# One half of look-ahead more for the first stage, patches in two transfers a unit, and rows doubled by VectorE instead of DMA

## The reference

```python
x = (x - mean) / (1e-06 + std)            # per patch and channel
x = x / math.sqrt(P)
x = _conv2d(x, conv1_w, conv1_b)          # 3 -> 64 channels, 3x3
residual = x
x = _group_norm(x, gn1_g, gn1_b)
x = jax.nn.gelu(x, approximate=False)
x = _conv2d(x, rconv1_w, rconv1_b)        # 64 -> 64, 3x3
x = _group_norm(x, gn2_g, gn2_b)
x = jax.nn.gelu(x, approximate=False)
x = _conv2d(x, rconv2_w, rconv2_b)        # 64 -> 64, 3x3
x = residual + x
x = _conv2d(x, proj_w, proj_b, stride=P, pad=0)   # 64 x 16 x 16 -> 192
```

## Time and profile before

| | us |
|---|---|
| median of 3 runs | 2082.0 |
| lowest, highest | 2076.85, 2090.18 |
| profiled execution, its own time | 2084.01 |
| its span, first to last instruction | 2082.2 |
| mean granted TensorE clock in it | 0.90 |

### The profile page before, as it was taken

The page is one execution under the profiler, slowest core; times in us unless marked ns, Lnnn a source line. Parts: engine busy times, 40 slices in busy tenths (PEclk is TensorE's granted clock), DMA queues, the critical chain, the costliest instruction groups (busy, mean ns, idle before and its releaser), DMA issues. The chain is left out here.

```text
span 2082.2 us, 45356 instructions
## 1 busy us (share of the span) xinstructions
PE 1634.7 (79%) x13560; PEld 1054.4 (51%) x13560; DVE 1224.6 (59%) x4296; ACT 947.6 (46%) x2114; POOL 907.6 (44%) x2183
## 2 busy tenths in 40 slices
PE   7899956777877687777877777687778775798899
PEld 2344423334655455545654555365545554665556
DVE  8876756775656556555665556565565555148240
ACT  3466535554444444444445444444444442032442
POOL 2000036665555555545555555455555552024220
PEclk9999989998989889989998999899888997897789
DMA  5522242223333333333333333333333337620000
GB/s 148 175 83 81 82 172 73 73 73 99 101 92 81 96 92 102 82 91 96 101 84 93 97 94 93 79 104 95 92 86 98 101 90 196 164 50 1 1 1 12
DMA packets 120494, 188.61 MB, mean 91 GB/s; under 512 B 22575, under 2 KB 90350, under 8 KB 120198
## 3 DMA queue, kind: packets, MB, share of 16 engines
q1 hardware_dynamic: 120326, 186.41, 33.5%
HBM read 103.06 MB, written 19.69 MB: 59 GB/s over the span
## 5 line engine op out<-in xcount | busy, mean ns | idle before, releaser
L499 PE MATMUL rc<-sb_acts,sb_rwd 128*64 128x512 f16 x1764 | 651.0, 446 | 336.2 <-DMA sb_acts<-sb_hst 336.1
L500 PE MATMUL rc<-sb_acts,sb_rwd 128*64 128x512 f16 x1764 | 652.2, 446 | 0.0
L414 ACT ACTIVATE sb_f32q<-c,sb_gsh,sb_gsc 128x128 f32<-128x128 f32 x788 | 297.0, 458 | 573.0 <-POOL sb_gsh L368 573.0
L499 PEld LDWEIGHTS rc<-sb_acts,sb_rwd 128*64 128x64 f16 x1764 | 193.1, 124 | 466.5 <-DMA sb_acts<-sb_hst 381.3
L357 POOL TENSOR_TENSOR sb_tmp<-sb_mst 128x4 f32<-128x4 f32 (+1 forms) x296 | 84.6, 286 | 756.3 <-DVE sb_mst L782 756.2
L362 POOL TENSOR_TENSOR sb_tmp<-sb_tmp,sb_half_neg 128x4 f32<-128x4 f32 (+1 forms) x296 | 386.7, 1306 | 23.2
L423 ACT ACTIVATE sb_g2f<-rc,sb_gsh,sb_gsc 128x128 f32<-128x128 f32 x784 | 296.8, 469 | 165.7 <-POOL sb_gsh L368 154.3
L499 PE MATMUL rc<-sb_acts,sb_rwl 128*64 128x512 f16 x1176 | 367.2, 394 | 3.8 <-issue 3.4
L500 PE MATMUL rc<-sb_acts,sb_rwl 128*64 128x512 f16 x1176 | 366.7, 394 | 0.0
L553 PE MATMUL pj<-sb_wall,sb_arena 128*64 128x384 f16 x1792 | 317.7, 357 | 18.8 <-DMA sb_wall<-w_lo 9.9
L782 DVE TENSOR_REDUCE sb_mst<-st 128x8 f32<-128x16 f32 (+1 forms) x296 | 52.6, 178 | 463.0 <-PE st L541 463.0
(11 more groups left out here) (161 smaller groups left out, 2573.8 us busy)
## 6 DMA issues: line engine op xcount, KB each, us to landing
sb_acts<-sb_hst SPq DMA_DIRECT2D x788, 78.8 KB, 2.1
sb_wall<-w_lo SPq DMA_DIRECT2D x56, 528.0 KB, 3.9
sb_im<-x_planes SPq DMA_DIRECT2D x300, 60.7 KB
sb_wall<-w_lo SPq DMA_DIRECT2D x28, 480.0 KB, 3.7
sb_im<-x_planes SPq DMA_DIRECT2D x300, 30.3 KB
sb_f32q<-in_proj SPq DMA_DIRECT2D x12, 576.0 KB, 4.5
sb_arena<-in_proj SPq DMA_DIRECT2D x12, 576.0 KB, 4.8
w_lo<-sb_arena SPq DMA_DIRECT2D x1, 6144.0 KB, 17.0
```

The costliest lines, as they stand in the source:

```text
L414: ins = nc.scalar.activation(g1f[:, q * Q + m, :], c1[q][:, m * HALF:(m + 1) * HALF], ACT.Gelu, bias=gsh[q][:, m:m + 1], scale=gsc[q][:, m ...
L499: nc.tensor.matmul(out[0:CH, :], w_odd, x_odd, start=(n == 0), stop=(n == 14))
L500: yield nc.tensor.matmul(out[CH:128, :], w_even, x_even, start=(n == 0), stop=(n == 14))
```

## The change

**Look-ahead.** The first stage is one half further ahead: in the time of half k, VectorE takes the statistics of half k+3 and splits half k+2, TensorE issues `means` of half k+3 and `conv1` of half k+4, ScalarE does `gelu1` of half k+2. The loop's length is the same; one more half is done in the prologue. `conv1` of half k+4 goes to the bank of the same q, and the wait for a unit's patches moves from q = 1 to q = 0.

**Doubling.** `double` is gone from SyncE. Behind its low part, `split1` copies the two halves of `hst[q]` to both halves of the partitions with four `tensor_copy` of 64 partitions x 630 elements, float16. `split1` no longer waits for transfers out of `hst`. The second-stage moments and `split2` now stand behind these copies.

**Patches.** `x_planes` has 18 planes (high, low, high again) instead of 12, written by three DMAs and six of zeros; `load_im` is two DMAs of 54 partitions instead of three of 24 and three of 12, the same bytes. `w1s` is in that order too, by twelve small DMAs.

```diff
--- before.py
+++ after.py
@@ -36,7 +36,7 @@
 FU = E // U
 RUN = (U - 1) * PAD + 8 * WD + P
 PLANE = (NPAT + 2 * U + 1) * PAD
-KA, KC = 72, 108
+KC = 108
 WS = 64.0
 EPS = 1e-5
 TR = 55
@@ -74,7 +74,7 @@
 
 
 
-    scr = nc.dram_tensor("x_planes", (12, PLANE), F16)
+    scr = nc.dram_tensor("x_planes", (18, PLANE), F16)
     wlod = nc.dram_tensor("w_lo", (128, HALF * E), F16)
     with ExitStack() as ctx:
         def sb(name, shape, dt=F32):
@@ -218,8 +218,9 @@
             sp.dma_start(xt, a["x"].rearrange("c p w n -> p c w n")).then_inc(s_xld, 16)
 
             sp.wait_ge(s_wprep, W_READY)
-            sp.dma_start(w1s[0:KA, :], w1hl[0:KA, 0, :]).then_inc(s_w1s, 16)
-            sp.dma_start(w1s[KA:KC, :], w1hl[KA:KC, 1, :]).then_inc(s_w1s, 16)
+            for at in range(0, KC, 18):
+                sp.dma_start(w1s[at:at + 12, :], w1hl[at:at + 12, 0, :]).then_inc(s_w1s, 16)
+                sp.dma_start(w1s[at + 12:at + 18, :], w1hl[at + 12:at + 18, 1, :]).then_inc(s_w1s, 16)
 
             def fold_io(i, p, last):
                 n = 2 * i + p
@@ -239,26 +240,24 @@
             for c in range(C):
                 sp.dma_start(xs.rearrange("(r w) (c n) -> r c w n", w=7, c=C)[:, c], xt[:, c]).then_inc(s_scr, 16)
             sp.wait_ge(s_xhl, 13)
-            for h in range(2):
-                sp.dma_start(bass.AP(tensor=scr, offset=h * 6 * PLANE, ap=[[7 * PAD, ROWS], [PLANE, 6], [1, 7 * PAD]]),
+            for k, h in enumerate((0, 1, 0)):
+                sp.dma_start(bass.AP(tensor=scr, offset=k * 6 * PLANE, ap=[[7 * PAD, ROWS], [PLANE, 6], [1, 7 * PAD]]),
                              xhl[:, 6 * h:6 * h + 6, :]).then_inc(s_scr, 16)
             sp.wait_ge(s_zero, 1)
             for n, k in ((NPAT, U), (NPAT + U, U), (NPAT + 2 * U, 1)):
-                sp.dma_start(bass.AP(tensor=scr, offset=n * PAD, ap=[[PLANE, 12], [1, k * PAD]]),
-                             zt[:, 0:k * PAD]).then_inc(s_scr, 16)
+                for at, planes in ((0, 12), (12, 6)):
+                    sp.dma_start(bass.AP(tensor=scr, offset=at * PLANE + n * PAD, ap=[[PLANE, planes], [1, k * PAD]]),
+                                 zt[0:planes, 0:k * PAD]).then_inc(s_scr, 16)
             def load_im(u, p):
-                for kx in range(3):
-                    sp.dma_start(im[p][24 * kx:24 * kx + 24, 0:RUN],
-                                 bass.AP(tensor=scr, offset=u * (U * PAD) + kx,
-                                         ap=[[PLANE, 12], [WD, 2], [1, RUN]])).then_inc(s_im[p], 16)
-                    sp.dma_start(im[p][KA + 12 * kx:KA + 12 * kx + 12, 0:RUN],
-                                 bass.AP(tensor=scr, offset=u * (U * PAD) + kx,
-                                         ap=[[PLANE, 6], [WD, 2], [1, RUN]])).then_inc(s_im[p], 16)
+                for up in range(2):
+                    sp.dma_start(im[p][54 * up:54 * up + 54, 0:RUN],
+                                 bass.AP(tensor=scr, offset=u * (U * PAD) + up * WD,
+                                         ap=[[1, 3], [PLANE, 18], [1, RUN]])).then_inc(s_im[p], 16)
 
             with sp.Fori(3, FU // 2 - 1) as i:
                 for p in range(2):
                     fold_io(i, p, False)
-            sp.wait_ge(s_scr, 16 * 8)
+            sp.wait_ge(s_scr, 16 * 12)
             load_im(0, 0)
             load_im(1, 1)
             for p in range(2):
@@ -266,13 +265,6 @@
             sp.wait_ge(s_wlo, 2 * FU)
             sp.dma_start(wlod.ap(), b1[:, 0:HALF * E]).then_inc(s_wst, 16)
             sp.sem_inc(s_emb, 32)
-
-            def double(k, p, q):
-
-                sp.wait_ge(s_sp1h, k + 1)
-                for row, half in ((0, 0), (0, 1), (1, 1), (1, 0)):
-                    sp.dma_start(acts[p][64 * half:64 * half + 64, row, q * Q * PAD + WD:(q + 1) * Q * PAD],
-                                 hst[q][64 * row:64 * row + 64, WD:Q * PAD]).then_inc(s_dup[p][q], 16)
 
             def store_tokens(lo):
                 sp.dma_start(emb[bass.ds(lo, 64), :], tok[0:64, :]).then_inc(s_emb, 16)
@@ -291,15 +283,12 @@
                         u = g * GU + 2 * j + p
                         sp.wait_ge(s_c1, 2 * u + 3)
                         load_im(u + 2, p)
-                        double(2 * u + 1, p, 1)
-                        double(2 * u + 2, 1 - p, 0)
                         if not first and 2 * j + p < NCH:
                             load_chunk(g, 2 * j + p)
                 if not first:
                     sp.wait_ge(s_pjr, g + 1)
                     store_tokens((g - 1) * G)
 
-            double(0, 0, 0)
             over_groups(sp, group)
 
             def load_colour(m):
@@ -332,7 +321,6 @@
             sp.wait_ge(s_pjr, GROUPS + 1)
             store_tokens((GROUPS - 1) * G)
             sp.wait_ge(s_emb, 32 * GROUPS + 32)
-            sp.wait_ge(s_dup[0][0], 64 * (UNITS // 2 + 1))
             sp.wait_ge(s_wr, 32)
 
         @block.gpsimd
@@ -370,14 +358,15 @@
             def pair(u0, j, first):
                 for p in range(2):
                     u = u0 + p
-                    norm(0, 0, 2 * u + 2)
+                    norm(0, 1, 2 * u + 3)
                     if not (first and p == 0):
                         norm(1, N2[1 - p], u - 1)
-                    norm(0, 1, 2 * u + 3)
+                    norm(0, 0, 2 * u + 4)
 
             pool.wait_ge(s_padz, 3)
             norm(0, 0, 0)
             norm(0, 1, 1)
+            norm(0, 0, 2)
             over_groups(pool, lambda g, b, first: over_units(pool, g, pair, first))
             norm(1, N2[1], UNITS - 1)
 
@@ -437,7 +426,7 @@
                         u = u0 + p
                         for q in range(2):
 
-                            gelu1(2 * u + 1 + q, 1 - q, not (first and p == 0 and q == 0))
+                            gelu1(2 * u + 2 + q, q)
                             if first and 2 * p + q < 3:
                                 continue
                             if head and 2 * p + q == 3:
@@ -453,6 +442,7 @@
 
             act.sem_inc(s_g2, 4)
             gelu1(0, 0, False)
+            gelu1(1, 1, False)
             group(0, 0, True)
             act.wait_ge(s_wst, 16)
             with act.Fori(0, (GROUPS - 1) // 2) as i:
@@ -597,15 +587,15 @@
                 woven(6)
                 pe.wait_ge(s_dup[p][q], 64 * (pairs_done + 1))
                 woven(1)
-                means(0, N1[q], 2 * u + q + 2, u - (q == 0) if k2 else 0)
+                means(0, N1[1 - q], 2 * u + q + 3, u - (q == 0) if k2 else 0)
                 woven(3)
-                if q == 1:
-                    pe.wait_ge(s_im[p], 96 * (pairs_done + 2))
-                pe.wait_ge(s_g1, 2 * u + q + 2)
-                conv1(1 - q, 1 - p if q == 0 else p)
+                if q == 0:
+                    pe.wait_ge(s_im[p], 32 * (pairs_done + 2))
+                pe.wait_ge(s_g1, 2 * u + q + 3)
+                conv1(q, p)
                 woven(3)
                 if q == 0 and k2:
-                    means(1, N2[1 - p], u - 1, 2 * u + q + 3)
+                    means(1, N2[1 - p], u - 1, 2 * u + q + 4)
                 woven(2).then_inc(s_rc, 1)
 
             def group0(g, b, first):
@@ -627,20 +617,23 @@
             pe.sem_inc(s_c1, 1)
             pe.sem_inc(s_pc, 2)
             pe.sem_inc(s_pj, 1)
-            pe.wait_ge(s_w1s, 32)
+            pe.wait_ge(s_w1s, 192)
             pe.wait_ge(s_rowz, 4)
-            pe.wait_ge(s_im[0], 96)
+            pe.wait_ge(s_im[0], 32)
             pe.wait_ge(s_tev, 3 * FU)
             pe.wait_ge(s_wlo, 2 * FU)
             conv1(0, 0)
             conv1(1, 0)
             means(0, 0, 0, 0)
             means(0, 1, 1, 0)
-            pe.wait_ge(s_im[1], 96)
+            pe.wait_ge(s_im[1], 32)
             pe.wait_ge(s_g1, 1)
             conv1(0, 1)
+            means(0, 0, 2, 0)
+            pe.wait_ge(s_g1, 2)
+            conv1(1, 1)
             over_groups(pe, group)
-            means(1, N2[1], UNITS - 1, 2 * UNITS + 2)
+            means(1, N2[1], UNITS - 1, 2 * UNITS + 3)
             for c in range(NCH):
                 chunk_waits(GROUPS, c)
                 last = run(project(0, CHS[c], CHS[c] + CHN[c]))
@@ -751,7 +744,7 @@
             ins.then_inc(s_padz, 1)
             dve.wait_ge(s_tps, FU)
             dve.wait_ge(s_padz, 3)
-            dve.wait_ge(s_scr, 16 * 8)
+            dve.wait_ge(s_scr, 16 * 12)
             v.sem_inc(s_rd[0], 1)
             v.sem_inc(s_rd[1], 1)
             v.sem_inc(s_pjr, 1)
@@ -793,6 +786,9 @@
                 v.tensor_copy(hi, src).then_inc(s_sp1h, 1)
                 dve.wait_ge(s_sp1h, k + 1)
                 v.tensor_tensor(lo, src, hi, ALU.subtract).then_inc(s_sp1, 1)
+                for row, half in ((1, 1), (1, 0), (0, 0), (0, 1)):
+                    v.tensor_copy(acts[p][64 * half:64 * half + 64, row, q * Q * PAD + WD:(q + 1) * Q * PAD],
+                                  hst[q][64 * row:64 * row + 64, WD:Q * PAD]).then_inc(s_dup[p][q], 16)
 
             def split2(k, q, buf, slot):
 
```

(22 more changed lines are left out.)

## The result

The changed kernel takes 2204.5 us (median of 4; 2193.5 to 2219.7) beside 2080.4 for the kernel before: ratio 1.059, 95% interval 1.052 to 1.067. Forecast were 1888 us and a range of 1800 to 2020. The change makes the kernel slower, by a mechanism that was not among the rivals. The profiled execution took 2193.5 (span 2191.7), the lowest of the four.

A forecast was written before the change was run, and what follows sets the result against it. TensorE was held by late doubling transfers in SyncE's queue; afterwards VectorE would be fullest. 2082 - 202 (84 units in groups 1 to 6, 15.1 to 12.7 us) + 0 (group 0) + 8 (ends) = 1888 us, range 1800 to 2020.

The forecast's parts named there:

- the price of the patch loads: Patch loads of a unit, covered by about three halves (some 18 us) until conv1: priced at nothing.
- The unit of 12.7 us: A pair of halves in groups 1 to 6, then 15.1 us: 6.6 + 5.5, plus 0.6 for small waits.
- GpSimd's and ScalarE's slack: Three norms need 10 us in 12.7; even half's GELU ends at 12.3, the split wants it at 12.7 + 0.1.
- GpSimd held up by the copies: VectorE's copies keep GpSimd out, three norms grow by up to 2.8 us, unit 14.1: 2020 us; chance 0.13.
- the copy: Each of VectorE's four copies a half, 630 elements on 64 partitions: 0.35 us, near the value by bytes.
- the rival of 1800 us: VectorE's copies cost about 0.24 us each (short and overlapped), unit 11.8 us: 1800 us; chance 0.15.
- those of 0.49 and 0.84: Copy at the CAST's rate (0.49 us): 1999 us, chance 0.12; one element at a time (0.84): 2273, chance 0.07.
- nothing is won: TensorE's gap goes, but it stops at means(1) for as long and its clock falls again: no gain; chance 0.03.
- Group 0: Token stage's first 28 halves, no projection woven in: VectorE's 11.9 us and some waits against 12.5, change 0.
- The fold, +8: One more plane store and three more zero stores delay the projection load, holding the fold: +8 us.
- the prologue, 0: One more half before the loop, but the first duplicate no longer waits for a transfer: 0.
- VectorE over 85% busy and a clock near 1.0: Signs of a right forecast in groups 1 to 6: VectorE then 59% busy, TensorE's granted clock then 0.90.

The follow-up runs named there:

- E1: The changed kernel with each unit's weight chunk load issued one unit later, behind the next patch loads: 2007.3 us, ratio 0.963 to the kernel before.
- E2: The changed kernel with the patch loads' source running over 18 planes outermost instead of 3 shifts (nine engines): 2000.2 us, ratio 0.960 to the kernel before.
- E4: The changed kernel with the six patch loads of the kernel before; look-ahead and VectorE's copies stay: 2193.4 us, ratio 1.054 to the kernel before.
- E9: The kernel before with the look-ahead only; DMA doublings, six patch loads and chunk place as before: 2158.5 us, ratio 1.035 to the kernel before.
- E7: The kernel before with VectorE's four copies in place of the doubling DMAs, nothing else changed: 1976.5 us, ratio 0.949 to the kernel before.
- E3: The changed kernel with E1's later chunk load and E2's 18 planes outermost together: 1992.8 us, ratio 0.955 to the kernel before.
- E6: E3 with the odd half's `split2` moved behind the next half's first-stage moments: 1915.2 us, ratio 0.920 to the kernel before.
- E5: E3 with the doubling given back to SyncE's DMAs and VectorE's copies out: 1887.6 us, ratio 0.909 to the kernel before.
- E8: E5 with the odd half's `split2` moved behind the next half's first-stage moments: 1786.8 us, ratio 0.861 to the kernel before.
- E10: The kernel before with only the change's two patch loads a unit (three engines); DMA doublings, no look-ahead: 1965.5 us, ratio 0.941 to the kernel before.
- E11: E10 with the patch source laid out so that nine engines carry each load: 1860.9 us, ratio 0.892 to the kernel before.
- E12: E11 with the odd half's `split2` later; DMA doublings, no look-ahead: 1801.1 us, ratio 0.864 to the kernel before.

## Why the prediction was wrong, point by point

**The step that failed** is the price of the patch loads: "they have about three halves (some 18 us) until conv1 of the unit. Priced at nothing for that cover". Three halves is what the buffers allow. The queue allows less: `load_chunk` stands in front with a wait of its own, so the loads leave at the end of an odd half. I counted what lies in SyncE's queue by its length (2.4 us a unit, right: 1.68 + 0.33) and not by what it waits for. The cover was 11 us before, seen in the earlier trace rows (1007.95 to 1019.10); with the look-ahead, which moves `conv1` a half forward, it is 2.7. The landing, taken from no row at all, was 6.5, some 2.5 of them behind the chunk. The price was 2204.5 - 1992.8 = 212 us; E1 and E2 each take nearly all of it away, E4 and E9 bring it up with the old transfers, and E4 against E7 shows it with the look-ahead as the only difference. The text did name the sign ("if TensorE waits for the patch loads"), but gave it neither a mechanism nor a chance.

**The unit of 12.7 us** is 13.8 where that wait is mended (E3): 84 x 1.1 = 92 of the 105 us that are left to 1888, group 0 (13.2 instead of 12.5) being another 10. The term that was mis-sized is GpSimd's and ScalarE's slack, "that fits by 0.4 us". It left out the high part (L420, 0.63 us and a start of 0.14) between the GELU and the split, and GpSimd's second-stage norm in E6's lines takes 4.0 us instead of 3.4. VectorE then waits 1.6 us. E6 gives back 78 us by moving the split out of the loop; that the loop accounts for all of the 92 is not shown.

**GpSimd held up by the copies**, the rival of 2020 us, came out far too large. In E6's lines L352 takes 0.44 us beside the CAST and ends just behind it, L354 0.66 beside the subtract, where the next norm's take 0.20 each; beside the first copy L356 takes 0.28. So most of the longer norm is the CAST and the subtract, which the kernel before has too, and 0.08 us is the copies. GpSimd's busy time grows by 21, 13, 50 and 16 us in the four pairs that differ only in who doubles the rows (before and E7, E9 and E4, E5 and E3, E8 and E6), so by 0.1 to 0.5 us a unit, not 1.4. The Trainium skill (SBUF — State Buffer, "SBUF: two separate sides") has the fast modes of VectorE lock the shared ports; the CAST's row, which I had called undecided, agrees.

**Right: the copy.** Forecast 0.35, measured 0.324; by bytes, not by elements. The four elements per cycle of the Trainium skill (VectorE: DVE Perf Modes, "The perf-mode tier table") gave 0.33, and the trace agrees. Four of them take 1.39 to 1.42 us, so no overlap, by which the rival of 1800 us fell, as did those of 0.49 and 0.84.

**Right: the wait for `acts` goes whole**; no such row is left in after's list. But "nothing is won" (0.03) is what came, and worse, though by another wait than its `means(1)`: one for the patches, of about the old length (280 us for 336), with the same fall of the clock.

**Group 0** was put at no change; it took 9 us more.

**The fold, +8, was about right, and the prologue, 0, was not.** The added stores held the queue about as long as I had allowed (six zero stores take 12.98 us where three took 6.25), and VectorE's wait behind them grew from 4.5 to 9.3 us:

```profile
89.41 12.98 SPq L249 DMA_DIRECT2D x_planes<-sb_arena  x6
...
107.95 0.77 DVE L673 TENSOR_SCALAR sb_acts<-sb_f32q 128x1152 f16<-128x1152 f32 x1 [9.29 <-DMA sb_f32q<-in_proj]
```

The first `conv1` of all starts at 278.06 us instead of 271.79: +6.3. In E10, without the look-ahead, these 6 us are still there two halves later (296.16 instead of 289.94). In after the same half's `conv1` starts at 290.51, 0.6 us later than before: the new prologue gives most of it back. So the two terms together left next to nothing of the 8.

**VectorE over 85% busy and a clock near 1.0** were to show the forecast right; after had 71% and 0.84. E3, without the new wait, has 84% and 0.98 over 1166 us of groups 1 to 6, so these two steps nearly hold once the patches come in time. The idle time behind which I had the clock fall, put at 3 us, was 3.46 in its row.

## What to carry to other kernels

When an order is moved ahead, list for each load not how long its buffer is free but when its queue reaches it: every wait that stands in front of it in an in-order queue, and when that wait ends in the profile. A queue that is mostly empty can still be the bound. And let a copy move to an engine only after pricing what else would unload the queue: here two well-spread loads in place of six (E11) took 11% off without a single copy, and one `split2` moved into the next half (E8, E12) took 3 to 5% more.

## What the runs showed of the hardware

- Two loads of 54 rows with an outermost source dimension of 3 moved at 72 to 83 GB/s, three packets in flight; the same bytes with 18 outermost reached 233 GB/s, with mostly seven to nine. By the time of the whole kernel the order of two dimensions in an access pattern was worth 204 us (E2) and 105 us (E11 against E10).
- Behind a gap of 3.78 us `conv1` took 0.63 us (1.2 GHz), behind one of 1.23 us 0.40 (2.4 GHz).
- The fourth of the small transfers right behind such loads landed 4.4 us after its issue with 3 outermost (E10), 3.1 with 18 (E11), 2.1 behind the six old loads (before).
- A 16-bit copy of 64 x 630 took 0.324 us. A GpSimd operation of 0.20 us that began beside a CAST took 0.44 and ended just behind it.
